# A graph kernel in which the edge counts move from the sort's permutations to the sorted tiles and the pair counts, with 80 instead of 112 gathers beside the typed tables

## What is computed

```python
x = layernorm(x + arma(x, edge_index, ...))       # 2 x 2 steps, three stacks, batch norm
x = layernorm(x + gcn(x, edge_index, W, b))       # sums over edges with 1/sqrt(degree) on both sides
x = layernorm(x + rgcn(edge_index, edge_type_9, x, weights, biases))
x = layernorm(x + neighbour(x, edge_index, ...))  # plain sums over edges
```

```python
seg = concatenate([edge_type * n + edge_index[0], (edge_type + R) * n + edge_index[1]])
count = segment_sum(ones, seg, 2 * R * n).reshape(2 * R, n, 1)
for l in range(2):
    agg = segment_sum(output[srcs], seg, 2 * R * n).reshape(2 * R, n, -1)
    hidden = output @ W[-1] + b[-1]
    for r in range(R):
        for inv in (0, 1):
            s = r + R * inv
            hidden = 2.0 * (hidden + agg[s] @ W[s] + count[s] * b[s]) / maximum(count[s], 1)
    output = relu(hidden) if l == 0 else hidden
```

## Time and profile before

| what | us |
|---|---|
| median of 3 runs | 4872.72 (4871.97 to 4880.41) |
| profiled execution, its own time | 4870.48 |
| its span | 4869.1 |
| sort by destination (rank, permute, end) | 16 to 281 |
| sort by source | 281 to 563 |
| staircase, pairs | 563 to 591, 591 to 805 |
| exact sum of x | 805 to 905 |
| typed tables, first layer | 2190 to 2396 |
| typed sum, first layer | 2396 to 3512 |
| tables and sum, second layer | 3519 to 3725, 3725 to 4736 |

### The profile page before, as it was taken

One profiled execution on the slowest core, in us unless ns is written; L12 is line 12 of the kernel. 1 busy time (PEld: TensorE's weight loads), 2 busy tenths in 40 slices (PEclk: granted clock), 3 DMA queues, 4 the chain that ended last, 5 costly groups with the idle time before them and its releaser, 6 DMA issues. The chain is left out here.

```text
span 4869.1 us, 56148 instructions
## 1 busy us (share of the span) xinstructions
PE 3319.2 (68%) x16061; PEld 2567.1 (53%) x16062; DVE 2278.0 (47%) x3880; ACT 1443.6 (30%) x2832; POOL 1749.4 (36%) x1969
## 2 busy tenths in 40 slices
PE   6979776999997999896465564554855433433359
PEld 3545423689995969683254454444633333323248
DVE  8979996244545425564343333333444212211134
ACT  5848586456666636540000000000000000000005
POOL 0000012011110102016356656666064666666631
PEclk8989898999998999998655555555676655555579
DMA  3000056388884849555311111111053111111115
GB/s 139 0 1 0 7 209 215 138 275 290 292 290 151 290 141 314 175 193 208 126 41 45 45 37 43 46 45 45 29 187 110 45 45 45 46 46 47 47 36 197
DMA packets 161460, 569.88 MB, mean 117 GB/s; under 512 B 46176, under 2 KB 54721, under 8 KB 160908
## 3 DMA queue, kind: packets, MB, share of 16 engines
q1 hardware_dynamic: 89494, 394.83, 23.6%
q0 software_dynamic: 71408, 172.45, 12.1%
q10 hardware_dynamic: 390, 0.60, 0.0%
HBM read 405.06 MB, written 162.66 MB: 117 GB/s over the span
## 5 line engine op out<-in xcount | busy, mean ns | idle before, releaser
L2027 PE MATMUL ps_sum_rgcn<-gathered_rgcn,select_sum_rgcn 128*128 x3328 | 984.5, 428 | 643.6 <-issue 605.9
L2027 PEld LDWEIGHTS ps_sum_rgcn<-gathered_rgcn,select_sum_rgcn 128*128 128x128 f32 x3328 | 756.4, 296 | 725.0 <-issue 722.1
L1943 POOL DMA_INDIRECT gathered_rgcn<-by_dst,row x782 | 739.6, 946 | 412.0 <-issue 217.7
L1609 PE MATMUL ps_sum_arma<-pair_counts_f_sum_arma,parts_sum_arma 128*128 128x448 f32 (+1 forms) x3850 | 852.7, 373 | 13.8 <-ACT pair_counts_f_sum_arma L1650 13.8
L1609 PEld LDWEIGHTS ps_sum_arma<-pair_counts_f_sum_arma,parts_sum_arma 128*128 128x128 f32 x3850 | 708.2, 190 | 68.1 <-issue 14.4
L1943 POOL DMA_INDIRECT gathered_rgcn<-by_src,row x558 | 527.8, 946 | 385.7 <-issue 150.9
L2066 ACT COPY acc_rgcn<-ps_sum_rgcn 128x128 f32<-128x128 f32 x100 | 26.6, 266 | 2069.6 <-PE ps_sum_rgcn L2027 1285.4
L2103 DVE TENSOR_TENSOR select_sum_rgcn<-one_hot_sum_rgcn,ps_coef_sum_rgcn 128x2048 f32<-128x2048 bf16 x52 | 119.0, 2288 | 762.5 <-PE ps_sum_rgcn L2027 471.5
L1488 POOL DMA_DIRECT2D rows<-parts_sum_arma x275 | 153.5, 559 | 882.0 <-DVE parts_sum_arma L1697 841.3
L1959 PE MATMUL ps_got_sum_rgcn<-factor_parts,turned_sum_rgcn 128*128 x832 | 183.3, 223 | 309.7 <-DVE turned_sum_rgcn L2080 214.0
L2080 DVE COPY turned_sum_rgcn<-ps_turn_sum_rgcn 128x1024 bf16<-128x1024 bf16 x104 | 71.7, 690 | 655.8 <-DMA params_norm_h<-in_L_gnn_beta 434.9
(11 more groups left out here) (459 smaller groups left out, 5179.5 us busy)
## 6 DMA issues: line engine op xcount, KB each, us to landing
blocks_arma_mid<-pairs SPq DMA_DIRECT2D x125, 800.0 KB, 6.4
axT_arma<-pairs SPq DMA_DIRECT2D x100, 800.0 KB, 6.1
pair_counts_arma_sum<-pairs SPq DMA_DIRECT2D x50, 800.0 KB
rows<-parts_sum_arma POOLq DMA_DIRECT2D x275, 128.0 KB, 5.5
by_src<-rows_rgcn_tables SPq DMA_DIRECT2D x50, 576.0 KB
by_dst<-rows_rgcn_tables SPq DMA_DIRECT2D x50, 576.0 KB
exact<-whole_pairs SPq DMA_DIRECT2D x25, 800.0 KB, 3.3
pairs<-whole_pairs POOLq DMA_DIRECT2D x25, 800.0 KB, 5.5
```

The lines of the kernel that those rows point to most:

```text
L1609: last = nc.tensor.matmul(ps[:, g, 0:here.stop - here.start], half(part), counts[:, n % 2, here].bitcast(F32R), start=t == 0 and part == 0 ...
L1943: nc.gpsimd.indirect_dma_start(got[:, n % PLACES, :], None, table, bass.IndirectOffsetOnAxis(ap=o.row[:, n % C:n % C + 1], axis=0)).then_i ...
L2027: nc.tensor.matmul(ps[:, bass.ds(slot, P)], select[:, parity, u, :], rows[:, bass.ds(place, D)], start=False, stop=False, skip_group_check ...
```

## The change

1. **Permutations.** The third product goes from both sorts, with the group operand. For key 1 local goes too, and DVE makes 14 of the 16 high columns instead of 8. For key 0 DVE makes local and a type operand of 9 columns, and 10 high columns; PE multiplies local by type into the count bank at an address loaded from `count_at` (16 values a turn). These are the edges of the list sorted by destination, so this gives the counts by destination.
2. **Degrees.** `degree_stage` goes; its operations move into the end stage of key 0. The spreading of the factors along rows moves from the rank stage to the staircase.
3. **Staircase.** The list of heavy nodes moves to fixed slots of the exact sum of x. The turned lists become three (the type is added), a second set of products picks the type of each item's edges, and `item_at` holds the count address times 65536 plus the span address.
4. **Pairs.** Each item gets a second product, of the source operand by a 9-column type operand, into the eighth bank: the counts by source. Both addresses are taken from the one loaded number.
5. **Gathers.** `EARLY` becomes 48 + 32 = 80 in both layers.

```diff
@@ Permute.run_stage, DVE
                     compare(self.place, o.slot_in, P).then_inc(self.placed, 1)
-                    compare(self.chunk, o.chunk_in, C)
-                    compare(self.local, o.local_in, P)
+                    if not o.key:
+                        compare(self.local, o.local_in, P)
+                        compare(self.type, o.type_in, R)
                     dve.wait_ge(self.placed, i + 1)
...
-                    compare(self.group, o.group_in, self.G).then_inc(self.made, 1)
+                    compare(self.chunk, o.chunk_in, C).then_inc(self.made, 1)
@@ Permute.run_stage, PE
+                    if not o.key:
+                        count_at = nc.values_load_multi_w_load_instructions(
+                            o.count_at[0:1, bass.ds(i * U, U)], engines=(PE,), min_val=2 * SPAN,
...
+                        if not o.key:
+                            nc.tensor.matmul(banks[:, bass.ds(count_at[u], R)], self.local[e, parity, pair, :, at],
+                                             self.type[e, parity, pair, :, at], start=False, stop=False,
+                                             skip_group_check=True)
...
-                        nc.tensor.matmul(self.ps[:, 2, 0:self.G], self.local[e, parity, pair, :, at],
-                                         self.group[e, parity, pair, :, at], start=False, stop=False).then_inc(self.moved, 1)
@@ staircase_stage, DVE
+            then(nc.vector.tensor_scalar(item_tile[:, :], item_tile[:, :], float(R * (COUNTS + 1) // SPAN), None, ALU.mult))
+            then(nc.vector.tensor_tensor(item_tile[:, :], item_tile[:, :], tile_at[:, :], ALU.add))
+            nc.vector.tensor_scalar(q.item_at[:, :, 0:DOZEN], item_tile[:, :].rearrange("p (n a) -> p n a", a=DOZEN),
                                     float(SPAN), None, ALU.mult)
@@ pair_counts_stage, DVE, once in 16 items
+                    nc.vector.tensor_tensor(
+                        typed[:, n // V % 2, :, :, :],
+                        q.type_at[:, n:n + V].rearrange("p (a b) -> p a b", b=2)[:, :, None, :].to_broadcast([P, V // 2, R, 2]),
+                        q.steps[:, None, 1:R + 1, :].to_broadcast([P, V // 2, R, 2]), ALU.is_equal)
@@ pair_counts_stage, PE, each item
-                    nc.tensor.matmul(ps[:, bass.ds(table[u % DOZEN], SPAN)], source[:, u // V % 2, u % V // 2, :, u % 2],
+                    block_at, count_at = (
+                        nc.s_assert_within(value, 0, most, skip_runtime_bounds_check_because="the two halves of an item's number")
+                        for value, most in ((table[u % DOZEN] & COUNTS, (SPANS - 1) * SPAN),
+                                            ((table[u % DOZEN] >> 16), (NT - 1) * R)))
+                    nc.tensor.matmul(ps[:, bass.ds(count_at + SPANS * SPAN, R)], source[:, u // V % 2, u % V // 2, :, u % 2],
+                                     typed[:, u // V % 2, u % V // 2, :, u % 2], start=False, stop=False, skip_group_check=True)
+                    nc.tensor.matmul(ps[:, bass.ds(block_at, SPAN)], source[:, u // V % 2, u % V // 2, :, u % 2],
                                      target[:, u % V, :], start=False, stop=False, skip_group_check=True).then_inc(multiplied, 1)
@@ typed layers
-EARLY = BEHIND + U * GROUP
+EARLY = BEHIND + 2 * U
```

More of the change, by code:

```diff
@@ L521, in end_stage @@
                 "closed", "step", "copied", "flipped", "evicted", "picked", "joined")
+            if not o.key:
+                deg = c.sb("degree", [P, NT])
+                has = c.sb("has_edges", [P, NT])
+                roots = c.sb("roots", [P, 2, NT])
+                rooting, rooted = c.sems("rooting", "rooted")
             block = c.block()
@@ L1048, in _ @@
             act.wait_ge(flipped, 1)
-            for n, less in enumerate((MIDDLE, 0)):
-                last = nc.scalar.activation(turned[:, n, :, :].rearrange("p h f -> p (h f)"), ps[0:Q4, 4 + n, :], ACT.Copy,
-                                            bias=float(-less))
+            for n, more in enumerate((-MIDDLE, 0, 1)):
+                last = nc.scalar.activation(turned[:, n, :, :].rearrange("p h f -> p (h f)"), ps[0:Q4, (4, 5, 7)[n], :], ACT.Copy,
+                                            bias=float(more))
             last.then_inc(moved, 1)
+            nc.scalar.copy(dinvT[:, :], ps[0:NT, 6, 0:P]).then_inc(kept, 1)
+            for g in range(FOURS):
+                tiles = four(g)
+                act.wait_ge(grouped, g + 1)
+                nc.scalar.copy(k.dinv_row[:, tiles.start * P:tiles.stop * P],
+                               ps[:, 6 + g % 2, 0:len(tiles) * P]).then_inc(evicted, 1)
         @block.vector
@@ L1209, in _ @@
             pe.wait_ge(zeroed, 1)
-            for g in range(SPANS):
+            for g in range(SPANS + 1):
                 nc.tensor.matmul(ps[:, g * SPAN:g * SPAN + SPAN], zero16[0:1, 0:P], zero16[0:1, :],
@@ L1524, in _ @@
                     sp.wait_ge(raised_too, n - RING + 1)
-                if exact is not None and n == CLONED:
+                if exact is not None and n == REPLACED:
                     sp.wait_ge(clone_made, 1)
@@ L1621, in _ @@
                 tables_up_to(min(n + 1 + AHEAD, 2 * n + 4))
+                if exact is not None and n == HEAVY + 1:
+                    pe.wait_ge(ready, 1)
+                    nc.tensor.matmul(ps[:, 7, 0:NT], ones[:, :], heavy16[:, :], start=True, stop=True)
+                    nc.tensor.matmul(ps[:, 7, LOW:LOW + NT], before[:, :], heavy16[:, :], start=True, stop=True).then_inc(counted, 1)
+                if exact is not None and n == LISTED + 2:
+                    pe.wait_ge(cloned, 1)
+                    for i in range(NT):
+                        last = nc.tensor.matmul(ps[:, 7, 2 * LOW:2 * LOW + 2], clone[:, i, :], place[:, i, :], start=(i == 0),
+                                                stop=(i == NT - 1))
+                    last.then_inc(placed, 1)
             if back:
@@ L1704, in _ @@
                     drain(n // NT - 1)
-                if exact is not None and n == CLONED - 4:
+                if exact is not None and n == CUTOUT:
                     dve.wait_ge(k.cloned, 32)
```

295 lines of the change are left out of this document (155 added, 140 removed).

## The result

The changed kernel takes 4906.53 us at the median of 5 runs (4891.95 to 4910.23) against 4872.72 for the kernel before: ratio 1.006, 95% interval 1.0041 to 1.008. Run again in a later session it was 1.0045 (1.003 to 1.0059). It is slower by about half a percent.

A forecast was written before the change was run, and what follows sets the result against it. DVE was taken to bound sorts and pair counts, PE's sequencer nearly as loaded in the latter. 4870.5 -58 -36 -9 +5 +155 -25 = 4902.5, with 2.2 for the median 4905; range 4772 to 4945, the forecast case's own 4850 to 4945.

The forecast's parts named there:

- Rival 1: Pair counts: mask and shift ride in the fused instruction, some 10 ns each; stage 251 us, total 4802; chance 0.25.
- three waits: Pair counts: PE's sequencer waits once for each four items, 0.3 us each, so three times in a dozen.
- The forecast of +155: Pair counts: at 0.44 us an item and 7.4 a dozen, the stage takes 354 us instead of 199.
- Each of the two products has its own fused address step: Pair counts: wide and narrow product of an item each need a fused register instruction, 0.12 us each.
- PE is late next: Sort by destination: DVE falls to 5.74 us a turn, PE needs 5.9; with some wait the turn is 6.0.
- the 0.6 us of exposed load: Sort by source: of each turn's load of 16 register values, 0.6 us is exposed, making the turn 7.0 us.
- part of the first layer's stage can take them: Typed sums: the first layer's sum absorbs part of the 32 returning gathers (45 us of POOL's time); net -25 us.
- a net of nothing in the second layer: Second typed layer: moving 32 gathers from tables to sum nets 0 us, with 30 to 34 saved in the tables.
- its own sign of being wrong: Prediction is wrong if mask and shift cost no own instruction, or sum stages change by over 30 us with the gathers.
- No load of PE here is under 1102 ns: Pair counts: said against the skill's floor of about 600 ns a register load, which would make the stage 24 us shorter.
- The forecast's low bound of 4850: Whole kernel: lower end of the forecast case's own range, down by 46 us for one shared fused step.

The follow-up runs named there:

- the shared address: Changed kernel with one count address for a dozen items and a type operand 27 columns wide: 4788.49 us, ratio 0.9753 to the kernel before.
- the kernel with the remainder: Changed kernel with the mask (AND 65535) of the pair counts written as a remainder by 65536: 4873.62 us, ratio 1.0003 to the kernel before.

## Why the prediction was right, and where it was not

**The total.** 4905 was forecast and 4906.5 measured, which flatters the working. The sum itself was made against the profiled execution, where it gives 4902.5 against 4891.9, and the profiled run happens to lie 15 under its median. Even these 10 us are what is left of larger misses of opposite sign: the gathers gave 18 us less than forecast, the pair counts cost 8 less, the sort by source gained 8 more, and 11 came in stages where nothing was forecast. That the total came out so near is luck; the loss itself and its cause are not.

**Pair counts.** The bound was named rightly: the sequencer, which the table of busy time doesn't show, goes from nearly as loaded as DVE to the only limit. Leaving out one product, changing one operator and sharing one address each moved the stage, by 92, 29 and 137 us. The stage was forecast at 354 us and took 354.6 from its first to its last record, but its terms were mis-sized. I had two lone operations and two plain fused steps, 0.44 us an item; the trace has one lone operation (0.092 to the next start), one plain step (0.12) and one step with the shift (0.159), 0.371 us. That is 40 us less over 576 items. Rival 1 was right in form for the shift, which rides in the fused instruction but adds 34 ns and not 10, and wrong for the mask. On the other side the load was too small: I took 1.2 us for the load and its address, and the mean load alone is 1.63 (the mean before is 1.63 also, but there DVE's pace hid it). With three waits at 0.97 together and the load's address at 0.1, a dozen is 12 x 0.371 + 0.97 + 1.63 + 0.1 = 7.15, times 48 is 343, of 354.6. The forecast of +155 became +147 because it was counted from DVE's 199 us of work, while the stage before takes 208.5 from first to last record.

**The second address.** "Each of the two products has its own fused address step" held in the changed kernel only because both addresses change with each item. Where one doesn't, the step vanishes, as the shared address shows.

**Sort by destination.** -58.7 against -58. That PE is late next, with some wait for DVE, is what the trace shows: turns of 5.89 and 6.34 us alternate, 6.1 on average and not 6.0, and ahead of every other one DVE waits for PE.

```profile
100.56 1.23 DVE L435 TENSOR_TENSOR place_one_hot_sort<-slot_in_sort,steps_sorts 125x2048 f16<-125x2048 f16 x1 [0.37 <-PE ps_sort L491]
...
106.46 1.22 DVE L435 TENSOR_TENSOR place_one_hot_sort<-slot_in_sort,steps_sorts 125x2048 f16<-125x2048 f16 x1
...
112.80 1.23 DVE L435 TENSOR_TENSOR place_one_hot_sort<-slot_in_sort,steps_sorts 125x2048 f16<-125x2048 f16 x1 [0.37 <-PE ps_sort L491]
```

A turn gained 2.25 and not 2.35. The forecast had nothing for two things outside the steady turns, which made up for it: one long turn near the start (10.6 us before, 7.7 after) and the time from the last turn's start to the end of the stage (16.7 before, 12.4 after).

**Sort by source.** -43.9 against -36. The step that failed is the 0.6 us of exposed load: the run without the load is no faster. Without that term DVE's 6.7 us rule the turn (PE has 6.4), and the same sum gives 26 x (8.35 - 6.7) = 43. The turns measure 6.69 and 6.75 us in the changed kernel.

**Small stages and staircase.** -10.2 against -9, and +6 against +5.

**Exact sum and the dense layers.** -10.8 where nothing was forecast. Most of this is scatter between profiles: the kernel before with 80 gathers has this part of the program as it was and takes 1376.1 us, and the nine profiles with the changed sorts lie between 1372.7 and 1379.7. So the list of heavy nodes moved there at no cost that shows, and no gain is shown either.

**Gathers.** -7 between the two profiles against -25 forecast, and -18 when done alone to the kernel before. The tables' part was underestimated (-37 a layer, not up to -34), the sums' part more so: +29 and +37. The step that failed is "part of the first layer's stage can take them" for most of the 32 gathers, and a net of nothing in the second layer. POOL's waits in the sum of the first layer, before and after, and then of the second:

```profile
POOL gathered_rgcn L1943 <- PE ps_sum_rgcn L2027: 107.2, 37, 22.1
POOL gathered_rgcn L1943 <- remote: 99.6, 50, 3.0
...
POOL gathered_rgcn L1997 <- remote: 111.2, 46, 8.3
POOL gathered_rgcn L1997 <- PE ps_sum_rgcn L2081: 82.9, 30, 21.6
```

```profile
POOL gathered_rgcn L1943 <- DMA blocks_arma_mid<-pairs: 70.5, 20, 5.0
POOL gathered_rgcn L1943 <- PE ps_sum_rgcn L2027: 64.4, 28, 8.2
...
POOL gathered_rgcn L1997 <- DMA blocks_arma_mid<-pairs: 91.2, 26, 5.2
POOL gathered_rgcn L1997 <- PE ps_sum_rgcn L2081: 39.8, 14, 10.0
```

POOL's waits for PE did fall by about 25 us in each layer between these two profiles, but its other waits rose by 12 and 21 us. Together they fell from 207 to 194 us in the first layer and from 135 to 131 in the second, so the stages could absorb about 13 and 4 us of the 40 that 32 gathers take, and grew by about the rest. How the profile shares the waits out varies: in the kernel with the remainder, which has the same gathers, the second layer has 84.9 us for PE and 55.8 for DMA, 141 together. The prediction named its own sign of being wrong here, a sum stage that grows by over 30 us: the second layer's did. The same sentence named a mask and shift that cost no instruction of their own; that came true of the shift alone.

At the start of the first layer's sum the first select operation comes 33 us into the stage and not 25, while POOL issues 48 gathers without a pause and not 16. With 80 early gathers it comes after 28 to 39 us in eight profiles, with 112 after 25 in two, with 48 (a burst of 84) after 29. That the burst holds DVE's small operations fits the tables stage, but the delay does not follow the length of the burst, and no run isolates it. The changed kernel's timeline of DVE at that place:

```profile
2403.05 0.69 DVE L2134 COPY turned_sum_rgcn<-ps_turn_sum_rgcn 128x1024 bf16<-128x1024 bf16 x1 [9.15 <-DMA params_norm_h<-in_L_gnn_beta]
2419.11 0.30 DVE L2138 TENSOR_TENSOR type_one_hot_sum_rgcn<-type,ps_iota_sum_rgcn 128x144 f32<-128x144 f32 x1 [15.37 <-DMA params_norm_h<-in_L_gnn_beta]
```

**Readings that were off.** DVE's idle time in the pair counts of the kernel before is 5.6 us, not 3.4: the earlier trace rows has 3.4 for the targets and 2.2 for the sources. "No load of PE here is under 1102 ns" holds for the 48 loads of the pair counts; in the typed sums of the same trace, loads of 16 values have a median of 1103 ns and records down to 3, and ACT's loads of 8 values in the pair counts take 537 ns at least. The comparison of 9 columns has 16 x 9 = 144 elements and took 0.226 us. The forecast's low bound of 4850 is 9 us under what its own term gives (4905 - 46 = 4859).

## What to carry to other kernels

Where an operand's address comes from a register, count the sequencer's steps for each item before adding one more: here 0.09 us for a lone operation and 0.12 to 0.16 for a fused one, against an item of 0.35 on DVE, and no engine looks full when the sequencer holds the stage. Arrange data so that the address doesn't change for a whole batch (a wider operand that carries the offset was cheaper than any decoding), and if something must be decoded, write it so that it goes into the fused step (the remainder instead of the mask gave 29 us). Moving work from one stage to another gains only what the receiving stage has in slack on the engine that paces it.

## What was not expected of the hardware

- The same value taken apart by a mask is a lone operation of 32 ns that costs 0.092 us; by a remainder it adds 33 ns to the fused one, 42 to 75. A right shift adds 34, 46 to 80.
- An address that doesn't change is worked out once and kept: 48 instead of 576 instructions. The product that uses it adds no step to the sequencer.
- A load of 16 values into PE's registers takes 1101 ns at least, of 28 values 1871. Loads that start within 3.5 us after the issue of an 800 KB store out of the same memory take up to 3.5 us; that the store is the cause is not shown.
